# Attention stage: products of probabilities and values in two double groups per four heads instead of one group in each head

## The reference, cut to what matters

```python
SIZE = 256; HEADS = 16; HEAD_DIM = 16              # per batch: t = s = 512
q = einsum('oc,bct->bot', Wq, target) + bq         # k, v likewise from the context
dot = einsum('bhdt,bhds->bhts', q, k) / sqrt(HEAD_DIM)
mask = target_mask[:, :, :, None] * source_mask[:, :, None, :]
dot = mask * dot - (1.0 - mask) * NEG
amap = softmax(dot, axis=-1) * mask
out = einsum('bhts,bhds->bhdt', amap, v)
```

## Time and profile before

| quantity | value |
|---|---|
| median of three runs | 3782.39 us |
| profiled execution, its time | 3785.51 us |
| profiled execution, its span | 3783.6 us |
| granted TensorE clock, mean | 0.940 |
| TensorE matmul busy | 3172.5 us (84%) |
| VectorE busy | 3054.2 us (81%) |
| ScalarE busy | 2540.9 us (67%) |
| GpSimd busy | 2143.7 us (57%) |

### The profile page before, as it was taken

One profiled execution on the slowest core, in us unless ns is written; L12 is line 12 of the kernel. 1 busy time (PEld: TensorE's weight loads), 2 busy tenths in 40 slices (PEclk: granted clock), 3 DMA queues, 4 the chain that ended last, 5 costly groups with the idle time before them and its releaser, 6 DMA issues. The chain is left out here.

```text
span 3783.6 us, 53475 instructions
## 1 busy us (share of the span) xinstructions
PE 3172.5 (84%) x16161; PEld 1878.1 (50%) x16194; DVE 3054.2 (81%) x2990; ACT 2540.9 (67%) x4872; POOL 2143.7 (57%) x1352
## 2 busy tenths in 40 slices
PE   6878888888888888888876478898898899859998
PEld 4666566656665666566655233343343333324444
DVE  1999998989989989899999377777787777638887
ACT  3878787877777877777776035565565556647777
POOL 1888887878888878788888123343243334210000
PEclk9989999999999999999996789999999999989999
DMA  4012101110121012101110445454553544331111
GB/s 151 3 57 70 71 14 58 70 71 12 59 71 71 12 60 70 69 10 63 71 65 1 123 134 153 137 158 134 161 160 114 171 149 128 102 100 42 44 44 37
DMA packets 157518, 311.41 MB, mean 82 GB/s; under 512 B 21969, under 2 KB 77393, under 8 KB 157089
## 3 DMA queue, kind: packets, MB, share of 16 engines
q1 hardware_dynamic: 152880, 299.46, 24.6%
q10 hardware_dynamic: 4352, 8.39, 0.6%
HBM read 216.11 MB, written 91.69 MB: 81 GB/s over the span
## 5 line engine op out<-in xcount | busy, mean ns | idle before, releaser
L681 DVE TENSOR_TENSOR_SCAN states<-states,bu 128x1024 f32<-128x1024 f32 x512 | 1173.7, 2292 | 188.4 <-POOL bu L612 107.2
L612 POOL TENSOR_TENSOR bu<-du,bc 128x1024 f32<-128x1024 f32 x512 | 1196.3, 2361 | 117.1 <-DVE states L681 113.9
L545 ACT ACTIVATE states<-dt,negA 128x256 f32<-128x256 f32 x2048 | 853.1, 464 | 440.6 <-DVE hc L693 380.4
L1162 ACT ACTIVATE pt<-s_ps 128x512 f32<-128x512 f32 x1024 | 573.4, 597 | 427.9 <-PE s_ps L1057 418.7
L1313 DVE TENSOR_REDUCE mmax<-s_ps 128x2 f32<-128x1024 f32 x512 | 624.4, 1223 | 288.0 <-PE s_ps L1048 272.8
L421 PE MATMUL y_ps<-id_sb,hc 128*128 128x128 f32 x4096 | 575.3, 286 | 143.3 <-DVE hc L693 143.2
L693 DVE TENSOR_TENSOR hc<-states,bc 128x1024 f32<-128x1024 f32 x512 | 626.8, 1224 | 52.3 <-DVE states L681 0.9
L421 PEld LDWEIGHTS y_ps<-id_sb,hc 128*128 128x128 f32 x4096 | 490.8, 147 | 308.1 <-DVE hc L693 262.6
L1057 PE MATMUL s_ps<-qst,kst 105*128 105x512 bf16 x1024 | 387.0, 392 | 13.1 <-ACT pt L1162 5.1
L1048 PE MATMUL s_ps<-kst,qst 102*128 102x512 bf16 x1024 | 325.3, 401 | 83.9 <-issue 42.7
L390 PE MATMUL proj<-xpad,diagW 128*128 128x256 f32 x1024 | 260.4, 388 | 42.1 <-ACT xpad L488 42.1
(11 more groups left out here) (153 smaller groups left out, 4529.3 us busy)
## 6 DMA issues: line engine op xcount, KB each, us to landing
bc<-bc_scratch SPq DMA_DIRECT2D x128, 512.0 KB, 4.7
stack_d<-parts SPq DMA_DIRECT2D x192, 256.0 KB, 3.0
w_raw<-in_w_ffn SPq DMA_DIRECT2D x32, 768.0 KB, 6.1
qst<-stack_d SPq DMA_DIRECT2D x64, 384.0 KB
kst<-stack_d SPq DMA_DIRECT2D x64, 384.0 KB
x<-xres SPq DMA_DIRECT2D x32, 512.0 KB, 3.5
xT_sb<-in_xT SPq DMA_DIRECT2D x16, 512.0 KB, 3.5
xres<-in_x SPq DMA_DIRECT2D x16, 512.0 KB, 3.7
```

Of the source, the lines that this page charges most:

```text
L545: a = act.activation(states[:, bank, first:first + SEQ], dt[:, t, :], ACT.Exp, scale=negA[:, t, c * NS + n:c * NS + n + 1])
L612: pool.tensor_tensor(bu[:, buf, :].rearrange("p (n l) -> p n l", n=NS), du[:, t % (2 * GRP):t % (2 * GRP) + 1, :].to_broadcast([P, NS, SEQ ...
L681: m = dve.tensor_tensor_scan(dst, dst, bu[:, BU_OF[k][0], half * 2 * SEQ:(half + n) * 2 * SEQ], 0.0, ALU.mult, ALU.add)
L1162: act.activation(pt[:, g % 2, u % HG, st, :], s2_ps[:, st % 2], ACT.Exp).then_inc(exp_done, 1)
```

## The change

In each body the values are issued in heads 1, 3, 5, ... 15 only, two groups in each: `st` = 0 and 1 in the second head of four, `st` = 2 and 3 in the fourth. The place inside the head (after the second `scores_exp`) stays, and so do all instructions, operands, waits and their order among the values.

```diff
                         if active(b):
                             scores_exp(b, par, u, tt)
-                        if tt == 1 and g >= 0 and active(b):
-                            values(b, par, g, u % HG)
-                        if tt == 1 and g < 0 and active(n):
-                            values(n, 1 - par, HGROUPS - 1, u % HG)
+                        if tt == 1 and u % 2 == 1:
+                            for st in (u % HG - 1, u % HG):
+                                if g >= 0 and active(b):
+                                    values(b, par, g, st)
+                                if g < 0 and active(n):
+                                    values(n, 1 - par, HGROUPS - 1, st)
                         if tt == 0:
                             shared_part(u - 1, 2)
```

## The result

The changed kernel takes 3834.12 us, the median of four runs (3831.58 to 3837.55), against 3783.52 for the kernel before in its four runs: a ratio of 1.0136, with a 95% interval of 1.0119 to 1.0154, so 50.6 us slower. The forecast was 3837.

The account below looks back on a forecast made before the run. TensorE was taken to be held in even heads by VectorE's read-out while odd heads grow: 5.7 + 0.27 - 2.2 = 3.8 us a body, 49 over bodies 1 to 13, +54 us in all; forecast 3837 us, range 3802 to 3862.

Parts of the forecast that it names:

- The bound: Even heads: without its group TensorE arrives earlier but waits for VectorE's read-out, 2.65 us into head 6.
- Odd heads: Eight odd heads each grow 0.90 us, 7.2 a body; after cover of 0.6 and 0.9, 5.7 remain.
- The gap at the edges: Around each value group: about 0.1 us on each side, paid once instead of twice in a double group.
- Even heads: Even heads shrink only to their next wait, saving 2.2 us a body where eight slots would be 8.7.
- Heads 11 to 13: Head 11's growth covered by head 12's wait, which saves nothing; 0.27 for copies and 0.9 for head 13, 1.17 together.
- The copies: Head 12: both value copies fall into GpSimd's L1267 and end 0.40 us after it; cost 0.27 us.
- the clock rival: Half-rate stretch after head 12's wait doubles, adding 15 times 1.7 us: 3862 us; chance 0.08.
- the cover of head 11's double group: All 0.9 us of head 11's growth is covered by head 12's long wait, which GpSimd times.
- The sum: Per body 5.7 + 0.27 - 2.2 = 3.8 us, 49 over bodies 1 to 13; together +54 us.
- The loop turns: At six loop turns the slow first head gives back 1 us in all.
- The first body and body 14: First body, no values in heads 0 to 3: about 1.5 us; body 14, no key and query projections: 2.5.
- Body 15: Last body, without row maxima and paced by exponentials: 1.5 us added.

Follow-up runs that it names:

- E1: Kernel before with double groups in heads 7 and 15 only, single groups in twelve other heads: 3802.15 us, ratio 1.0048.
- E2: Kernel before with double groups in heads 1 and 11 only, single groups in twelve other heads: 3781.63 us, ratio 0.9994.
- E4: Changed kernel with row maxima over 256 of 512 columns, the rest left out: 3727.82 us, ratio 0.9847 to the kernel before.
- E11: E10 with the double groups of the changed kernel: 3751.32 us, 22 us slower than E10.
- E3: Kernel before with row maxima over 256 of 512 columns, the rest left out: 3715.98 us, ratio 0.9817.
- E10: Kernel before with L1267 held until the value copies finish, context load a head earlier, shared-bank read-out ahead of the first row maximum: 3729.54 us, ratio 0.9847.
- E7: Kernel before with GpSimd's L1267 moved from head 12 to head 15, away from the value copies: 3734.78 us, ratio 0.9876.
- E8: Changed kernel with the same move of L1267 to head 15: 3775.71 us, 41 us slower than E7.
- E5: Kernel before with the eight double groups in even heads and none in odd heads: 3831.96 us, ratio 1.0127.

## Why the prediction was right

*The bound.* That TensorE is held in even heads by a chain on VectorE that its missing work can't shorten was the core of the argument. The changed trace shows the waits, E1 and E2 that equal double groups differ in price from head to head, and E4 and E11 that the price falls from 50.6 to 11.8 and 22 us when the read-out comes earlier. The totals hold other things too (loads, turns, body 15), so the sum over heads 2 to 14 of the table is the cleaner measure: double groups add 3.4 us a body there in the changed kernel, 0.7 from E3 to E4 and 1.6 from E10 to E11. From E7 to E8, with the long wait of head 12 gone but the read-outs as late as ever, they add 3.3, so the long wait of head 12 is not what sets the price.

*Odd heads.* The slot of a double group grew by 0.87 us (1.86 less 0.99); I took 0.90, and streams alone gave 0.86 to 0.88. The gap at the edges is thus paid once a pair instead of twice, about 0.2 us, and is the small thing it was taken for. Heads 1, 5, 7 and 15 grew by 0.70 to 0.74, 3 and 9 by 0.86: 4.6 us in sum, against 4.8 forecast for these six.

*Even heads.* Forecast 0.78, 0.19, 0.48, 0, 0.60, 0.05 and 0.07 for heads 0, 2, 4, 6, 8, 10 and 14; measured 0.78, 0.18, 0.38, -0.12, 0.41, 0.07 and 0.08, 1.8 in sum and not 2.2. Two things that I left out explain the three that were off. After a double group the second row maximum of the odd head starts late, so the first one of heads 6 and 8 starts 0.82 us into the head instead of 0.70, and the read-out behind it ends at 2.76 us instead of 2.65. And a product that comes out of a wait starts slowly. In head 4, where the reduction started on time, the first shared product starts 0.13 us after the read-out's end, not 0.08, and the score product behind it comes after 0.16 us instead of 0.11; in head 8 the second shared product comes after 0.32 us instead of 0.21.

*Heads 11 to 13.* Forecast 1.17 together (0.27 for the copies, 0.9 for head 13), measured 1.21, and that these agree is luck. The copies came out as written: both behind GpSimd's instruction, end 0.41 after it. Counted from the start of head 11, TensorE's wait ends at 12.12 us and not at 11.91, so this is 0.21 us. Head 13 grew by 0.35 only; it ran in part at the lower clock level before (4.59 us, where it takes 3.81 in E7 with the clock at 1.00) and less so after, and with the clock at 1.00 in both, from E7 to E8, it grows by 0.66. The other 0.65 us lie in head 12 behind the wait, where the copies no longer matter: the granted clock in head 12 of bodies 0 to 13 is 0.76 to 0.95 before, median 0.91, and 0.70 to 0.87 after, median 0.75. That is the clock rival, at less than half of its price, and I had left it out of the sum. I had also read head 12 off body 8, where it lasted 9.15 us; the median is 9.54. Last, the cover of head 11's double group isn't the wait of head 12, as I wrote, but mostly its own wait for ScalarE's copies of the maxima (E8).

*The sum.* 3.8 us a body forecast, 4.0 from the table. The attention grew by 54.0 us in the profiled executions from its first score product to its last, 54 forecast. That the two are equal is luck, as the terms outside these bodies were off and cancelled. The loop turns gave back 7.5 us where I had 1, and I had counted six turns where the trace has five. The first body and body 14 cost -0.1 and 1.3 us, not 1.5 and 2.5. Body 15, for which I had 1.5, cost 7.6 (46.6 to 54.2 us from its first to its last score product for exponentials): its clock fell, which I had thought of in head 12 only. So the mechanism of the heads was right, but that the total came within 3 us of 3837 owes something to luck. The windows of that body, first the changed kernel's, then that of before, and a double group in it:

```profile
3340.00:3394.00 54.00, 45.72 (x215) 12.28 (x215) 4.82 (x11) 36.33 (x70) 13.69 (x8) 0.87 0.13 43
```

```profile
3294.00:3341.00 47.00, 39.33 (x215) 10.52 (x217) 5.57 (x11) 36.25 (x70) 14.61 (x11) 1.00 0.15 49
```

```profile
3343.55 3.50 PE L1066 MATMUL pv_ps<-pt,vaug 128*32 128x512 f32 x16
...
3346.98 0.60 PE L1057 MATMUL s_ps<-qst,kst 105*128 105x512 bf16 x2
```

The granted clock was 1.00 in this body before and is 0.87 now. Ahead of the double group shown lies head 0, score products and one small transpose, in which TensorE waited 0.56, 0.59 and 0.20 us for exponentials. From 3340 to 3343.3 us the granted clock is 1.00, from 3343.4 to 3346.7 it is 0.50, and the double group, 1.86 us elsewhere, takes 3.43. This one body costs about as much in the experiments with all eight double groups in odd heads: it lasts 54.2 us in E4, 52.8 in E8 and 53.9 in E11, and 46.6 in each of E3, E7 and E10. So body 15 alone adds 7.6 us from E3 to E4, where the whole difference is 11.8, and 7.3 from E10 to E11, where it is 22; neither is a matter of read-outs.

Open: why E5's even heads got no cover is not explained by a run of its own. No run changes the clock stretch of head 12 by itself, and why the granted clock is lower there in the changed kernel and in E1 is not shown.

## What to carry to other kernels

When filler work is moved from one step to another, the step that loses it shrinks only to the next wait, while the step that gets it grows in full unless it waits somewhere itself (as head 11 did, with 0.27 us for 0.87); read for each step when the thing that is waited for is ready, and not which engine is busiest on average. Merging instructions to save a gap of 0.1 us at each edge paid here only where it put work into a wait: it cost 1.3% to 1.4% in all odd or all even heads and, with four groups put into the wait of head 12, gained 0.7%. Two engines that collide, as VectorE's copies and GpSimd's instruction did here with starts 0.13 us apart, were worth more: moving the one out of the way gained 1.2% (E7).

## What the runs showed that I had not expected

At each turn of the hardware loop TensorE stands still some 8 us ("issue"), and this is no constant. It was 42.7 us in five turns before and 35.2 after the change, 38.2 in E1, 42.8 in E2, 54.1 in E7 and 57.6 in E3: by and large, the faster the bodies, the longer the turn. E5 is out of line, with 41.3 us and bodies longer than E1's. In E3 that is 3.0 us more a turn, taken from what the two bodies between turns had gained. What TensorE waits for at the turn, no run here shows.

The other was body 15: with one group in each head the granted clock was 1.00 there, and with eight double groups in odd heads 0.87 to 0.90 (the changed kernel, E4, E8, E11), at 0.93 with them in even heads (E5). Two double groups in a body didn't do it: in E1 and E2 the clock stayed at 1.00 and the body took 46.9 and 47.0 us.
